# Gated delta-rule block: k turned to token rows by VectorE's 32x32 transposes and eight DMAs in place of TensorE's products with the identity, with a new order on all engines

## The chip, the cores and the metric

The kernel runs on one core of one Trainium2 chip, as one program. The metric is the device time of one execution in microseconds. Everything is float32.

## The reference

The input x is 16 sequences of 256 tokens by 256 channels. It is normalised over its channels and projected to q, k, v and z (32 heads of 64) and to two gates per head. q, k and v pass a causal convolution of four taps over time. q and k are scaled to unit length. Each head then runs a recurrence over the tokens with a 64x64 state, and the result is normalised, gated and projected back:

```python
def step(Sstate, xs):
    q_t, k_t, v_t, g_t, b_t = xs
    Sstate = Sstate * jnp.exp(g_t)[..., None, None]
    kv = jnp.einsum('bhk,bhkv->bhv', k_t, Sstate)
    delta = (v_t - kv) * b_t[..., None]
    Sstate = Sstate + k_t[..., :, None] * delta[..., None, :]
    o_t = jnp.einsum('bhk,bhkv->bhv', q_t, Sstate)
    return (Sstate, o_t)
...
o = o * lax.rsqrt(var + EPS) * norm_weight * jax.nn.sigmoid(z)
return o.reshape(Bsz, Sl, VDIM) @ w_out.T
```

Both the attention part and a gated feed-forward part (256 to 1024 to 256) are normalised and added to their input: `x = x + _layernorm(attn(_layernorm(x)))`, then the same with the feed-forward part.

## The kernel before

Stage 1 normalises x, transposes it and computes the gates. Stage 3 is the feed-forward part. Stage 2, the attention, takes most of the time and is all that the change touches. It has 64 steps: 8 groups of four heads by 8 spans of 512 tokens (two sequences). A step holds 16 tiles of 64 tokens by two head halves (G = 16), on 128 partitions.

In a step TensorE makes eight projections of 128x512 (`project`, L1313; outputs 0 and 1 are k, 2 and 3 are q, 4 and 5 are v, 6 and 7 are z). ScalarE does the first tap from PSUM and VectorE adds three more (`conv`, L1077) for k and v; for q, ScalarE makes the products and GpSimd adds them. k and q then lie with channels on partitions. `scores` (L1335) multiplies k with k and q per tile. The recurrence is done in chunks of 64 tokens, so a 64x64 triangular matrix has to be inverted per tile: VectorE solves its 16x16 diagonal blocks column by column (`substitute`, L1091, after two transfers through DRAM, a_d), and four rounds of small products join them (`join16_inner` to `join_outer`, L1348 to L1382), fed by two more transfers (z_d and x_d).

The chunks follow each other in a chain over c = 0 to 3: `key_state` (TensorE, L1384), `residual` (VectorE, L1145), `solve` (TensorE, L1393), `delta_out` (ScalarE, L933), `advance` (TensorE, L1403), `new_state` (VectorE, L1153), with `output` (L1413) beside them. After the last chunk come `square_o`, `add_squares`, `sum_squares`, `log_var`, `combine`, `gates`, `gated`, `project_out` and `accumulate`. The state starts anew in each step, so no step needs the state of another.

Token rows of k, that is tokens on partitions, are needed for the length of k (`squares`, `sum_k`, `norms`, `columns`) and for `kt`, the left operand of `advance`. In the kernel before they come from `k_tokens` (L1330): 32 products of a 64x64 block with the identity per half of a step, into a PSUM bank of which ScalarE takes squares and VectorE takes `kt`. Token rows of v are made without TensorE: VectorE transposes 32x32 blocks (`turn_v`, L1107, into v_x) and eight DMAs put the blocks in their places (`v_turned`, L712).

The order of the work is written out by hand for each engine in a function `turn(s)`, where s[k] is the step that is k turns old. All engines run their turns in this fixed order, and every dependency is a semaphore wait (`wait_for(eng, sem, step, count, back)`). SyncE issues every DMA, also in a written order (L720), with the waits in between on the same engine. Projections, scores, k_tokens, sum_squares and project_out share four PSUM banks (`ring`, L550); the others have banks of their own. `ap_mat`, `kt`, `z_t`, `v_r` and `q_g` are double, `gcrow`, `xT`, `k_tok` and `v_x` are single.

## Time and profile before

| | |
|---|---|
| time, median of 3 runs | 3149.84 us (3148.64 to 3151.75) |
| the profiled execution: its own time | 3143.98 us |
| its span, first to last instruction | 3142.2 us |
| VectorE busy | 2390.4 us (76%) |
| ScalarE busy | 1765.5 us (56%) |
| GpSimd busy | 1117.6 us (36%) |
| SyncE's DMA queue, share of 16 engines | 34.9% |
| mean granted TensorE clock | 0.988 |

The engine rows are sums of busy time over the whole span, so they mix the three stages. Granted clock 1.0 is 2.4 GHz and 0.5 is 1.2 GHz. TensorE's own row stands further down with the rows that the prediction uses.

### The profile page before, as it was taken

What the parts mean: (1) busy time and instruction counts of PE and PEld (TensorE: products, weight loads), DVE (VectorE), ACT (ScalarE), POOL (GpSimd) and SP (SyncE); (2) the same over time, 40 slices, a digit from 0 to 9 for tenths busy, and PEclk for the clock granted to TensorE, in tenths of its full rate; (3) what the DMA queues carried; (4) which work ended last, traced back from release to release, by engine and by line L of the source; (5) the groups of instructions that cost most, each with busy time, mean ns of one, the idle gap of its engine ahead of it and who ended that gap; (6) DMA issues with size and microseconds to landing.
All of it is one profiled execution on the core that took longest, in us unless ns stands there. A gap on an engine that the chain in (4) does not pass through costs nothing. (4 is left out here: it accounts for less than half of the span.)

```text
span 3142.2 us, 109422 instructions
## 1 busy us (share of the span) xinstructions
PE 3023.2 (96%) x46912; PEld 2040.8 (65%) x46912; DVE 2390.4 (76%) x5674; ACT 1765.5 (56%) x3306; POOL 1117.6 (36%) x904
## 2 busy tenths in 40 slices
PE   6799999999999999999999999999999999789998
PEld 3466666666666666666666666666766666655455
DVE  7578888888788878888878888887888888545644
ACT  5456666665666655666656566665566666333432
POOL 1444444444444444444444444444444444100000
PEclk9899999999999999999999999999999999899999
DMA  5333434344344433433344444333333334300000
GB/s 152 69 62 68 79 65 68 68 86 70 70 70 83 68 68 64 82 63 66 69 85 69 70 70 86 67 67 67 73 69 64 67 69 69 75 14 27 27 21 14
DMA packets 1027793, 208.77 MB, mean 66 GB/s; under 512 B 977904, under 2 KB 998768, under 8 KB 1026160
## 3 DMA queue, kind: packets, MB, share of 16 engines
q1 hardware_dynamic: 1027312, 201.78, 34.9%
q8 instruction: 373, 6.11, 0.8%
q14 instruction: 108, 0.88, 0.1%
HBM read 120.13 MB, written 39.58 MB: 51 GB/s over the span
## 5 line engine op out<-in xcount | busy, mean ns | idle before, releaser
L1317 PE MATMUL bank<-xT,w_sb 128*128 128x512 f32 x2048 | 996.9, 615 | 15.7 <-DVE kq L1082 9.2
L1317 PEld LDWEIGHTS bank<-xT,w_sb 128*128 128x128 f32 x2048 | 359.7, 190 | 355.9 <-issue 311.9
L773 POOL TENSOR_TENSOR kq<-kq,product 128x510 f32<-128x510 f32 (+2 forms) x384 | 437.3, 1146 | 108.9 <-ACT kq L869 94.3
L1082 DVE SCALAR_TENSOR_TENSOR v_c<-bank,cw,v_c 128x510 f32<-128x510 f32 (+2 forms) x384 | 286.3, 746 | 23.0 <-ACT v_c L869 13.1
L1082 DVE SCALAR_TENSOR_TENSOR kq<-bank,cw,kq 128x510 f32<-128x510 f32 (+2 forms) x384 | 283.7, 739 | 23.7 <-ACT kq L869 14.6
L761 POOL TENSOR_TENSOR dec_ap<-gcrow,gcb 128x1024 f32<-128x1024 f32 x64 | 121.8, 1903 | 502.4 <-DMA gcb<-gcb_d 502.4
L1342 PE MATMUL bank<-kq 64*64 64x128 f32 x4096 | 277.9, 270 | 3.4 <-DVE ap_mat L1135 1.9
L1446 PE MATMUL bank<-wo,u_sq 128*128 128x256 f32 x1024 | 261.4, 399 | 11.4 <-DVE u_sq L1168 11.4
L1097 DVE TENSOR_TENSOR prod_un<-a_un,x_un 128x15 f32<-128x15 f32 (+7 forms) x960 | 216.1, 225 | 60.3 <-DMA a_un<-a_d 42.2
L873 ACT ACTIVATE product<-bank,cw 128x512 f32<-128x512 f32 x384 | 257.1, 688 | 2.1 <-PE bank L1317 2.1
L1424 PEld LDWEIGHTS bank<-ap_mat,delta 64*64 64x64 f32 x4096 | 218.3, 135 | 47.0 <-issue 47.0
L777 POOL TENSOR_SCALAR z_tmp<-z_tmp 128x512 f32<-128x512 f32 x128 | 79.2, 619 | 469.4 <-ACT z_tmp L863 464.0
L1424 PE MATMUL bank<-ap_mat,delta 64*64 64x64 f32 x4096 | 243.2, 220 | 0.0
L934 ACT COPY delta<-bank 128x256 f32<-128x256 f32 x256 | 95.4, 373 | 260.4 <-PE bank L1399 260.4
L1342 PEld LDWEIGHTS bank<-kq 64*64 64x64 f32 x4096 | 228.2, 133 | 5.6 <-issue 5.6
L1101 DVE TENSOR_TENSOR x_un<-x_un,prod_un 128x15 f32<-128x15 f32 (+7 forms) x960 | 201.0, 209 | 32.9
L869 ACT ACTIVATE kq<-bank,cw 128x512 f32<-128x512 f32 x256 | 176.9, 691 | 79.5 <-PE bank L1317 77.9
L1446 PEld LDWEIGHTS bank<-wo,u_sq 128*128 128x128 f32 x1024 | 188.3, 194 | 39.2 <-DVE u_sq L1168 12.5
L1422 PE MATMUL bank<-q_g,state 64*64 64x64 f32 x3072 | 199.5, 221 | 1.1 <-ACT delta L934 1.1
L786 POOL TENSOR_TENSOR q_g<-kq,gcrow 128x512 f32<-128x512 f32 x128 | 188.5, 1494 | 0.8 <-PE bank L1424 0.6
L1422 PEld LDWEIGHTS bank<-q_g,state 64*64 64x64 f32 x3072 | 186.4, 134 | 1.5 <-issue 1.3
L1389 PEld LDWEIGHTS bank<-state,kq 64*64 64x64 f32 x3072 | 112.0, 135 | 98.6 <-issue 98.6
(169 smaller groups left out, 5767.3 us busy)
## 6 DMA issues: line engine op xcount, KB each, us to landing
xT<-xT_d SPq DMA_DIRECT2D x64, 512.0 KB, 3.9
gcrow<-gcrow_d SPq DMA_DIRECT2D x128, 256.0 KB, 4.4
v_r<-v_x SPq DMA_DIRECT2D x512, 64.0 KB
a_d<-ap_mat SPq DMA_DIRECT2D x256, 64.0 KB, 3.6
z_t<-z_d SPq DMA_DIRECT2D x256, 64.0 KB, 2.5
w_sb<-in_w_qkvz SPq DMA_DIRECT2D x8, 1024.0 KB, 6.6
x_un<-eye_un SPq DMA_DIRECT2D x64, 128.0 KB, 2.2
a_un<-a_d SPq DMA_DIRECT2D x64, 128.0 KB, 3.5
```

Of the source, the lines that this page charges most:

```text
L773: nc.gpsimd.tensor_tensor(t[:, :, d:SEQ], t[:, :, d:SEQ], prod[:, :, 0:SEQ - d], ALU.add).then_inc(tap_added[i], 1)
L786: ins = nc.gpsimd.tensor_tensor(q_g[m.par][:, a * GP:(a + 1) * GP, :], half_of(m, 1)[:, a, :].rearrange("p (g c) -> p g c", c=C), gcrow[:, ...
L869: nc.scalar.activation(dst, bank[:, :], ACT.Identity, scale=cw_two[m.grp % 2][:, s * TAPS + TAPS - 1:s * TAPS + TAPS]).then_inc(tap_done[s ...
L873: ins = nc.scalar.activation(products[i % 4], bank[:, :], ACT.Identity, scale=cw_two[m.grp % 2][:, w:w + 1])
L1082: ins = nc.vector.scalar_tensor_tensor(t[:, :, d:SEQ], src[:, :, 0:SEQ - d], cw_two[m.grp % 2][:, w:w + 1], t[:, :, d:SEQ], ALU.mult, ALU.add)
L1097: own.need(own.mark(nc.vector.tensor_tensor(prod, a_un[:, j + 1:B, j:j + 1].broadcast_to([P, rows, wid]), x_un[:, j:j + 1, 0:wid].broadcas ...
L1101: ins = nc.vector.tensor_tensor(rest, rest, prod, ALU.subtract)
L1317: ins = nc.tensor.matmul(bank[:, :], w_two[m.grp % 2][:, h, s * P:(s + 1) * P], xT[:, h, :], start=(h == 0), stop=(h == HT - 1))
L1342: ins = nc.tensor.matmul(bank[half, i * P:(i + 1) * P], kq[half, k, s // 2, t0:t0 + C], kq[half, k:q + 1:q - k, s // 2, t0:t0 + C], start= ...
L1422: nc.tensor.matmul(o, state[c % 2][half, i, :], q_g[m.par][half, g, :], start=True, stop=False)
L1424: ins = nc.tensor.matmul(o, delta[half, i, :], p_t[m.par][half, g, :], start=(c == 0), stop=True)
L1446: ins = nc.tensor.matmul(bank[:, t * HID:(t + 1) * HID], u_sq[:, a, (2 * k + t) * P:(2 * k + t + 1) * P], wo[m.grp % 2][:, a, :], start=(a ...
```

## The change

k's token rows are made as v's are. `turn_k` transposes 32x32 blocks of k on VectorE into `k_tok`, and `k_turned` moves the blocks with eight DMAs into a new tile `k_r`. `squares` and `scale_k` read `k_r` in SBUF, and `squares`, `sum_k`, `scale_k` and `scale_v` each take a whole step in one instruction in place of two halves. `tokens` and `k_tokens` are gone from TensorE. `v_x` is gone too: v's blocks also pass through `k_tok`, so `turn_k` waits until v's DMAs of the step before have landed. `substitute` is split into its product and its subtraction. The order of every engine is new: the pipeline spans six turns (DEPTH) in place of four, and load_gates, x_out and identity_in stand elsewhere in SyncE's order. In the diff below, indentation is cut by 16 and lines left out are marked.

```diff
         prod_un = sb("prod_un", [P, 4 * B])
         x_row = sb("x_row", [P, G, C])
-        v_x = sb("v_x", [P, G, C])
+        k_r = sb("k_r", [P, G, C])
         p16 = sb("p16", [P, G, W2])
         x_top = sb("x_top", [P, G, W2])
         p1 = sb("p1", [P, G, W2])
...
-        DEPTH = 4
+        DEPTH = 6
...
-            return banks[(18 * m.off + place) % 4]
+            return banks[(2 * m.off + place) % 4]
...
+    def turned(dst, landed):
+
         for h in range(2):
             for f in range(2):
                 for t in range(2):
                     r, q = D * h + W2 * t, D * h + W2 * f
+                    sp.dma_start(dst[r:r + W2, :, W2 * f:W2 * f + W2], k_tok[q:q + W2, :, W2 * t:W2 * t + W2]) \
+                        .then_inc(landed, 16)
+
+    def v_turned(m):
+        turned(v_r[m.par], v_f_in)
+
+    def k_turned(m):
+        turned(k_r, k_f_in)
 
     def turn(s):
+        if s[5]:
+            wait_for(sp, mats_done[0], s[5], 1)
+            units_out(s[5])
+        if s[4]:
+            wait_for(sp, qg_done[0], s[4], 1, back=1)
+            load_gates(s[4])
+        if s[5]:
+            wait_for(sp, a_d_out, s[5], 64)
+            units_in(s[5])
+            wait_for(sp, vx_done[0], s[5], 1)
+            v_turned(s[5])
+        if s[4]:
+            wait_for(sp, kx_done[1], s[4], 1)
+            k_turned(s[4])
+        if s[5]:
+            wait_for(sp, zt_done, s[5], 1)
+            z_out(s[5])
+            x_out(s[5])
+            wait_for(sp, z_d_out, s[5], 16)
+            z_back(s[5])
+            wait_for(sp, x_d_out, s[5], 16)
+            x_back(s[5])
+        if s[3]:
+            wait_for(sp, proj_full[4], s[3], 1, back=1)
+            load_x(s[3])
+        if s[4]:
+            identity_in(s[4])
...
-    def squares(m, a, bank):
-        nc.scalar.activation(k_tok[:, a * GP:(a + 1) * GP, :], bank[:, :].rearrange("p (g c) -> p g c", c=C), ACT.Square).then_inc(ksq_done[a], 1)
+    def squares(m):
+        nc.scalar.activation(k_tok[:, :, :], k_r[:, :, :], ACT.Square).then_inc(ksq_done, 1)
...
-        ins = nc.vector.transpose(v_x[:, a * GP:(a + 1) * GP, :].rearrange("p g c -> p (g c)"), v_c[:, a, :])
+        ins = nc.vector.transpose(k_tok[:, a * GP:(a + 1) * GP, :].rearrange("p g c -> p (g c)"), v_c[:, a, :])
...
+    def turn_k(m, a):
+        ins = nc.vector.transpose(k_tok[:, a * GP:(a + 1) * GP, :].rearrange("p g c -> p (g c)"), half_of(m, 0)[:, a, :])
+        if a in kx_done:
+            ins.then_inc(kx_done[a], 1)
+
+    def sum_k(m):
+        nc.vector.tensor_reduce(sumk, k_tok[:, :, :], AX.X, ALU.add).then_inc(sumk_done, 1)
+
+    def scale_k(m):
+        nc.vector.tensor_tensor(kt[m.par][:, :, :], k_r[:, :, :], col(e_tail).broadcast_to([P, G, C]), ALU.mult).then_inc(kt_done, 1)
+
+    def scale_v(m):
+        nc.vector.tensor_tensor(v_r[m.par][:, :, :], v_r[m.par][:, :, :], col(br).broadcast_to([P, G, C]), ALU.mult).then_inc(vr_done, 1)
...
+        if s[4]:
+            wait_for(dve, ks_full[1], s[4], 1)
+            residual(s[4], 1)
+        if s[3]:
...
+        if s[4]:
...
+        if s[3]:
...
+        if s[5]:
+            wait_for(dve, op_full[0], s[5], 1)
+            accumulate(s[5], 0, ring(s[5], 2))
+        if s[3]:
...
+            sub_rest(s[3], 14)
+            wait_for(dve, v_f_in, s[3], 128)
+            scale_v(s[3])
+        if s[4]:
+            wait_for(dve, st_full[1], s[4], 1)
...
+            new_state(s[4], 1)
+            wait_for(dve, state_done[1], s[4], 1)
...
+            wait_for(dve, ks_full[2], s[4], 1)
+            residual(s[4], 2)
+        if s[2]:
...
+            conv(s[2], 4, ring(s[2], 0))
+        if s[5]:
+            wait_for(dve, op_full[1], s[5], 1)
+            accumulate(s[5], 1, ring(s[5], 3))
+        if s[4]:
+            wait_for(dve, st_full[2], s[4], 1)
+            new_state(s[4], 2)
+        if s[2]:
+            wait_for(dve, ksq_done, s[2], 1)
+            sum_k(s[2])
+        if s[4]:
+            wait_for(dve, ks_full[3], s[4], 1)
+            residual(s[4], 3)
+        if s[2]:
+            wait_for(dve, rk_done, s[2], 1)
+            wait_for(dve, rhs_done[3], s[2], 1, back=2)
+            columns(s[2])
+            conv(s[2], 5, ring(s[2], 2))
+            wait_for(dve, score_full[1], s[2], 1)
+            wait_for(dve, deca_done, s[2], 1)
+            wait_for(dve, o_full[3], s[2], 1, back=2)
+            matrices(s[2], 1, ring(s[2], 3))
+            wait_for(dve, score_full[2], s[2], 1)
+            matrices(s[2], 2, ring(s[2], 0))
+            wait_for(dve, score_full[3], s[2], 1)
+            matrices(s[2], 3, ring(s[2], 2))
+            matrices(s[2], 0, ring(s[2], 1))
+        if s[4]:
...
+            add_squares(s[4], 1)
...
+            add_squares(s[4], 0)
+        if s[2]:
+            scale_k(s[2])
+            turn_v(s[2], 1)
+            turn_v(s[2], 0)
+        if s[3]:
+            wait_for(dve, z16_done, s[3], 1)
+            turn_back(s[3])
+        if s[4]:
...
+            combine(s[4], 1, ring(s[4], 1))
+        if s[1]:
...
+            conv(s[1], 0, ring(s[1], 0))
+        if s[4]:
...
+            combine(s[4], 0, ring(s[4], 0))
         if s[1]:
...
             conv(s[1], 1, ring(s[1], 1))
+        if s[4]:
...
+            gated(s[4], 1)
...
+            gated(s[4], 0)
+        if s[2]:
+            wait_for(dve, x_un_in, s[2], 16)
+            wait_for(dve, a_un_in, s[2], 16)
+            sub_product(s[2], 0)
...
+            sub_rest(s[2], 6)
         if s[1]:
+            wait_for(dve, conv_done[0], s[1], 1)
+            wait_for(dve, v_f_in, s[1], 128, back=1)
+            turn_k(s[1], 0)
+            wait_for(dve, conv_done[1], s[1], 1)
+            turn_k(s[1], 1)
+        if s[2]:
+            sub_product(s[2], 7)
+        if s[3]:
+            wait_for(dve, st_full[0], s[3], 1)
+            new_state(s[3], 0)
+        if s[2]:
...
         if s[1]:
+            wait_for(dve, gc_in, s[1], 48)
+            tail(s[1])
+        if s[2]:
+            sub_product(s[2], 10)
...
-    def tokens(src, a, bank):
...
-    def k_tokens(m, a, bank):
...
+        if s[2]:
+            wait_for(pe, conv_done[1], s[2], 1)
+            project(s[2], 3, ring(s[2], 1))
+        if s[4]:
...
+            advance(s[4], 0)
+            wait_for(pe, qg_done[0], s[4], 1)
+            wait_for(pe, og_done[0], s[4], 1, back=1)
+            output(s[4], 0)
+            wait_for(pe, state_done[0], s[4], 1)
+            key_state(s[4], 1)
+        if s[5]:
+            wait_for(pe, z_exp[1], s[5], 1, back=-3)
+            wait_for(pe, og_done[0], s[5], 1)
+            project_out(s[5], 0, ring(s[5], 2))
+        if s[2]:
...
+            project(s[2], 6, ring(s[2], 3))
+        if s[4]:
+            wait_for(pe, rhs_done[1], s[4], 1)
+            solve(s[4], 1)
+        if s[2]:
+            wait_for(pe, z_exp[1], s[2], 1)
+            wait_for(pe, acc_done[0], s[2], 1, back=3)
+            project(s[2], 4, ring(s[2], 0))
+        if s[4]:
...
+            advance(s[4], 1)
+            output(s[4], 1)
+            wait_for(pe, state_done[1], s[4], 1)
+            key_state(s[4], 2)
+        if s[5]:
...
+            project_out(s[5], 1, ring(s[5], 3))
+        if s[4]:
+            wait_for(pe, rhs_done[2], s[4], 1)
+            solve(s[4], 2)
+        if s[2]:
...
+            wait_for(pe, z_exp[0], s[2], 1)
+            scores(s[2], 1, ring(s[2], 3))
+        if s[4]:
...
+            advance(s[4], 2)
+        if s[2]:
...
+            wait_for(pe, conv_done[4], s[2], 1)
+            scores(s[2], 2, ring(s[2], 0))
+        if s[4]:
+            wait_for(pe, state_done[2], s[4], 1)
+            key_state(s[4], 3)
+        if s[2]:
+            scores(s[2], 0, ring(s[2], 1))
+        if s[4]:
+            output(s[4], 2)
+            wait_for(pe, rhs_done[3], s[4], 1)
+            solve(s[4], 3)
+        if s[3]:
+            wait_for(pe, z_in, s[3], 64)
+            join16_inner(s[3])
+        if s[4]:
...
+            output(s[4], 3)
+        if s[2]:
+            wait_for(pe, conv_done[5], s[2], 1)
+            scores(s[2], 3, ring(s[2], 2))
+        if s[3]:
...
+            wait_for(pe, x_row_in, s[3], 64)
+            join16_outer(s[3])
         if s[1]:
...
+            wait_for(pe, mats_done[3], s[1], 1, back=1)
+            project(s[1], 0, ring(s[1], 0))
+        if s[4]:
...
+            sum_squares(s[4], 1, ring(s[4], 1))
+        if s[3]:
...
+            join_inner(s[3])
+        if s[4]:
...
+            sum_squares(s[4], 0, ring(s[4], 0))
         if s[1]:
+            project(s[1], 1, ring(s[1], 1))
+        if s[3]:
...
+            join_outer(s[3])
         if s[1]:
+            wait_for(pe, mats_done[0], s[1], 1, back=1)
+            wait_for(pe, comb_done[1], s[1], 1, back=3)
+            project(s[1], 2, ring(s[1], 3))
+            wait_for(pe, conv_done[0], s[1], 1)
+            project(s[1], 7, ring(s[1], 0))
+            wait_for(pe, comb_done[0], s[1], 1, back=3)
+            project(s[1], 5, ring(s[1], 2))
+        if s[3]:
...
+            solve(s[3], 0)
```

## Rows read from the trace of the kernel before

**Rows 1.** The page's busy times: us, share of the span, instructions.

```profile
PE 3023.2 (96%) x46912; PEld 2040.8 (65%) x46912; DVE 2390.4 (76%) x5674; ACT 1765.5 (56%) x3306; POOL 1117.6 (36%) x904
```

**Rows 2.** Windows: stretch, its length, busy us per engine, clock, DMA share, GB/s.

```profile
1200.00:1500.00 300.00, 298.79 (x5303) 208.36 (x5299) 244.63 (x570) 180.39 (x337) 131.05 (x105) 1.00 0.41 73
```

**Rows 3.** TensorE's timeline: start, duration, instruction; projections 0 and 2 of two steps.

```profile
196.15 3.60 PE L1317 MATMUL bank<-xT,w_sb 128*128 128x512 f32 x8
...
2646.23 3.60 PE L1317 MATMUL bank<-xT,w_sb 128*128 128x512 f32 x8
```

**Rows 4.** TensorE's timeline, parts of one turn in the middle.

```profile
1402.38 1.10 PE L1326 MATMUL bank<-masks,kq 64*64 64x64 f32 x32
1403.31 0.33 PE L1422 MATMUL bank<-q_g,state 64*64 64x64 f32 x4
...
1404.71 1.15 PE L1326 MATMUL bank<-masks,kq 64*64 64x64 f32 x32
1405.65 0.68 PE L1409 MATMUL bank<-delta,kt 64*64 64x64 f32 x16
1406.11 0.33 PE L1422 MATMUL bank<-q_g,state 64*64 64x64 f32 x4
...
1417.00 1.13 PE L1439 MATMUL bank<-u_sq,ones 128*128 128x512 f32 x2
1418.05 1.63 PE L1362 MATMUL bank<-p,x_row 64*48 64x32 f32 x64
1419.61 1.12 PE L1439 MATMUL bank<-u_sq,ones 128*128 128x512 f32 x2
1420.57 3.60 PE L1317 MATMUL bank<-xT,w_sb 128*128 128x512 f32 x8
1424.10 1.20 PE L1371 MATMUL bank<-z_t,ap_mat 32*32 32x32 f32 x64
...
1430.82 1.98 PE L1317 MATMUL bank<-xT,w_sb 128*128 128x512 f32 x4
1432.73 0.68 PE L1409 MATMUL bank<-delta,kt 64*64 64x64 f32 x16
1433.35 1.98 PE L1317 MATMUL bank<-xT,w_sb 128*128 128x512 f32 x4
...
1461.13 3.60 PE L1317 MATMUL bank<-xT,w_sb 128*128 128x512 f32 x8
```

**Rows 5.** TensorE's timeline at the end of stage 2, with idle time and releaser.

```profile
2737.94 0.68 PE L1409 MATMUL bank<-delta,kt 64*64 64x64 f32 x16 [0.56 <-ACT delta L934]
2739.22 0.68 PE L1389 MATMUL bank<-state,kq 64*64 64x64 f32 x16 [0.61 <-DVE state L1158]
```

**Rows 6.** Groups of VectorE: count, busy us, mean ns, idle us before.

```profile
L1124 DVE TENSOR_TENSOR v_r<-v_r,cols 128x512 f32<-128x512 f32 x128 | 106.1, 829 | 0.0
L1108 DVE STREAM_TRANSPOSE v_x<-v_c 128x512 f32<-128x512 f32 x128 | 89.6, 701 | 0.0
L1685 DVE TENSOR_TENSOR acc<-gcrow,dec_ap 128x1024 f32<-128x1024 f32 x7 | 8.6, 1225 | 0.7
```

**Rows 7.** Timelines of VectorE and GpSimd: scale_v's two halves, and mask.

```profile
1441.92 0.68 DVE L1124 TENSOR_TENSOR v_r<-v_r,cols 128x512 f32<-128x512 f32 x1
...
1450.88 0.98 DVE L1124 TENSOR_TENSOR v_r<-v_r,cols 128x512 f32<-128x512 f32 x1
...
1448.96 2.35 POOL L765 TENSOR_TENSOR dec_ap<-dec_ap,masks 128x1024 f32<-128x1024 f32 x1 [0.78 <-ACT dec_ap L853]
```

**Rows 8.** SyncE's timeline: DMA issues (start, duration, count).

```profile
1425.13 6.93 SPq L717 DMA_DIRECT2D v_r<-v_x  x8
...
1486.73 0.40 SPq L697 DMA_DIRECT2D z_d<-t_un  x1
1489.89 2.87 SPq L702 DMA_DIRECT2D z_t<-z_d  x4
1492.88 0.54 SPq L684 DMA_DIRECT2D x_un<-eye_un  x1
```

**Rows 9.** A window in which v's transfers end, columns as in rows 2.

```profile
1433.00:1433.50 0.50, 0.50 (x17) 0.43 (x12) 0.04 (x1) 0.50 (x2) 0.00 (x0) 1.00 0.23 34
```

578 lines of the change are left out of this document (188 added, 390 removed).

## The prediction, made before the changed kernel ran

> **What bounds the kernel now.** I read the page's busy times first: TensorE is busy for 96% of the span, VectorE for 76% [rows 1]. An average over three stages proves little, so next the windows: in a stretch in the middle of stage 2 TensorE is busy 298.79 of 300 us at granted clock 1.00 (2.4 GHz), VectorE 244.63, ScalarE 180.39, GpSimd 131.05, the DMA engines 41% [rows 2]. Then TensorE's timeline. Projections 0 and 2 stand side by side once per turn, so their start marks the turn: from 196.15 to 2646.23 lie 60 turns [rows 3], 2450.08 / 60 = 40.83 us each. An undisturbed one takes 1461.13 - 1420.57 = 40.56 [rows 4]; 0.27 a turn is lost to late arrivals. Nothing but TensorE's own work fills a turn, so what shortens TensorE's turn shortens the kernel, until another engine or a transfer is late.
>
> **What goes from TensorE.** Ends of products are modelled and overlap the next start, so I count from start to start. One k_tokens call: 1403.31 - 1402.38 = 0.93; the other 1405.65 - 1404.71 = 0.94 [rows 4]. Together 1.87 us a turn, and VectorE, ScalarE or a DMA must carry them.
>
> **What the new order saves on TensorE.** Wide products (128 rows by 256 or 512 columns) and small ones cost extra where they alternate. A lone projection takes 1432.73 - 1430.82 = 1.91. sum_squares alone takes 1418.05 - 1417.00 = 1.05, and sum_squares followed by two projections 1424.10 - 1419.61 = 4.49, against 1.05 + 2 x 1.91 = 4.87 apart: each join of two wide calls saves 0.19. On the other side of the border, advance takes 1433.35 - 1432.73 = 0.62 ahead of a wide call and 1406.11 - 1405.65 = 0.46 ahead of a small one: 0.16 more. So a wide run fewer is worth 0.35 us [rows 4]. The order before has ten wide runs a turn: projections 7, 3, 5, 6, 4 alone, projection 1, two project_out, sum_squares(1), and sum_squares(0) with projections 0 and 2. The new one has seven: projection 3; project_out(0) with 6; 4; project_out(1); 0 with sum_squares(1); sum_squares(0) with 1; 2 with 7 and 5. Three fewer, 1.05 us. Bounds: nothing, if project_out ahead of a projection doesn't pipeline as the row shows, and 1.35, if a pair saves 2 x 1.91 - 3.53 = 0.29 by itself.
>
> **What the new order adds on TensorE.** The chunk chain has two places where little stands between. With nothing between but output(0), key_state(1) must follow advance(0) by 2739.22 - 2737.94 = 1.28 us, since new_state(0) lies between [rows 5]. The old order had projection 7 there. The new one has only output(0), so advance 0.46 and output about as much, 0.92: a stall of 0.36, at most 0.5. For the other chunks I find cover: project_out(0) and projection 6 (3.6 us) over residual(1), projection 4 over delta_out(1), output(1) with its double products over new_state(1), project_out(1) over residual(2), scores over delta_out(2) and new_state(2).
> TensorE's turn then is 40.56 - 1.87 - 1.05 + 0.36 = 38.00 us.
>
> **VectorE.** Its busy time is 244.63 / 300 x 40.83 = 33.3 us a turn [rows 2]. Added: two transposes of 0.70, 1.40 [rows 6]. sum_k, scale_k and scale_v each become one instruction of 1024 columns. The nearest row with two SBUF operands of that width is 1.225 us, against two halves of 0.68 (0.83 for scale_v on average) [rows 6, 7]: about -0.13, -0.13 and -0.4. New busy time 34.0, with some 1.2 us between dependent instructions (my estimate) 35.2 of 38.0. That is tight: it leaves 2.8 us, and the order fixes where. VectorE waits for TensorE's chunk products (new_state(1), residual(2), new_state(2)) and, through o_full(3), for output(3) ahead of matrices(1): each holds some 0.3 to 1.1 us of it. From matrices(1) on VectorE runs without a wait through add_squares, scale_k, turn_v, turn_back, two conv, gated, seven columns of substitute and turn_k to new_state(0), on which key_state(1) waits. I put this loop (output(3), that row of VectorE's work, new_state(0), key_state(1) to output(3)) at 37.9 us, from the mean durations, give or take 0.4. So it ties with TensorE's own turn, and a lengthening there counts whole. I take +0.3 for it: 38.3. Bounds: 0, and +1.5 in the second rival.
>
> Here the rows speak of a port. scale_v's second half, started while mask ran on GpSimd (1448.96 for 2.35 us), took 0.98; its first half, with GpSimd idle, 0.68 [rows 7]. The Trainium skill (SBUF — State Buffer, SBUF: two separate sides) says that a VectorE instruction with two SBUF inputs and a GpSimd instruction that reads SBUF exclude each other for a whole instruction. By that rule, the trace agrees: mask ended at 1451.31, and the half ended 0.55 later. The rule speaks against the change, since scale_k read PSUM before and reads k_r in SBUF now; what it would do is the second rival.
>
> **ScalarE and GpSimd** have room: 180.39 / 300 x 40.83 = 24.6 and 17.8 us of 38 [rows 2]. squares becomes one 1024-wide call. It stands behind the wait for k_f_in, with delta_out(2), first_tap(5) and norms queued behind it, so a late k stops the chunk chain within 1 us.
>
> **SyncE and the DMAs.** v's eight take 6.93 us to issue, 1425.13 to 1432.06 [rows 8], and the engines are emptied by about 1433.3, since the share falls to 0.23 in the half microsecond from 1433.0 [rows 9]: 1.3 us after the issue. k's eight are alike: 8.2 us from kx_done to k_f_in. turn_k stands right ahead of new_state(0), and squares some 10.5 us later on ScalarE (behind TensorE's key_state(1), two wide runs of 3.6 and 1.9 and two small calls, and four ScalarE calls): 2 us to spare. turn_k also waits for v's DMAs, which read k_tok; I get them landed about 1 us before it. Behind k's eight on SyncE stand z_out, x_out, z_back, x_back, load_x and identity_in. From turn_k: 6.9 for the issue, 0.4 for z_out, 1489.89 - 1486.73 - 0.40 = 2.8 until it has landed, 2.9 for z_back [rows 8], some 2 to land, together 15.0. TensorE reaches join16_inner about 17 us after turn_k. Slack 2 us, cost 0. load_gates now stands between units_out and units_in: its three issues fall into the 3 us or so in which a_d lands, and a_un has about 1 us to spare before column 0; I cost it at nothing, and if that cover goes, each microsecond is one of VectorE's loop. The split of substitute changes no instruction. SyncE's own issue time grows by 6.9 to some 31 us with its waits, under 38. DMA share rises from 0.41 x 40.83 = 16.7 us of a turn to some 20 of 38.3 (estimate: eight DMAs of v took about 5 us at two thirds share).
>
> **Sum.** Turn 38.3, plus the 0.27 of late arrivals that I keep: 38.6. Gain 40.83 - 38.6 = 2.23, x 60 turns = 134 us. Filling and emptying the pipeline: a step waits on the same chain, k adds some 8 us of DMA beside a path that had room, and the first and last turns lose projections that they hadn't filled; I take +3 (bounds -8 and +20). 3143.98 - 134 + 3 = 3013 for the profiled execution. The median is 5.86 above the profiled one: 3019.
>
> **Rival 1, TensorE's order pays less and VectorE's loop binds.** Nothing from the wide runs (+1.05) gives a turn of 39.05, plus 0.27: 39.3, gain 1.5 x 60 = 92, time 3061. For: VectorE with 35.2 of 38 us leaves no room to reorder. Against: the 0.38 saved by a run of three is on the row.
>
> **Rival 2, the port.** scale_k and scale_v wait behind GpSimd instructions of 1.5 to 2.4 us, and conv and add_squares beside scale_q and differences. If 1.5 us of it falls in VectorE's loop: turn 37.9 + 1.5 = 39.4, plus 0.27, gain 1.16 x 60 = 70, time 3083. Against: scale_v stood in such a place and lost only 0.3 [rows 7].
>
> **Rival 3, slower: SyncE's order.** k's DMAs stand between turn_k and z_out. If the chain from turn_k to join16_inner grows from 15 us by more than its slack of 2, TensorE stands at z_in, join16_outer or ScalarE at k_f_in, each turn. It decides from 2 + (40.83 - 38.6) = 4.2 us more: then the kernel is no faster. With 6 us more (the chain 40% longer, the issue of eight DMAs held up by a ring that now serves 20 us of 38) the turn is 42.6, time 3143.98 + 1.8 x 60 + 6 = 3258. For: v's issues took 6.93 / 8 = 0.87 each and z_back's 2.87 / 4 = 0.72, so issues of the same size do get held up [rows 8]. Against: the DMA engines stay half idle.
>
> **Chances.** The forecast, 2995 to 3050: 0.58. Rivals 1 and 2, 3050 to 3105: 0.27. Below 2995: 0.06. Rival 3: 0.07. No change, when a wait I haven't seen eats the gain: 0.02. A change under 0.2% (6.3 us) can't be told from none. Faster 0.91, same 0.02, slower 0.07. Range 2990 to 3100.
>
> **What would show it.** Projection 0 to projection 0 some 38.6 us apart. Seven wide runs and no identity products. project_out(0) with projection 6 in 3.6 us start to start. An idle of about 0.4 before key_state(1) by new_state(0), and none above 0.3 elsewhere on TensorE. VectorE busy near 0.89 of a turn, transposes x256. scale_k at 1.2 us; 2 or more speaks for the port. squares waiting for k_r's DMA, or join16_inner for z_t's, speaks for rival 3. I am wrong if the turn is above 39 with TensorE waiting at a place not named here.

## The result, and the profile after

| | before | after |
|---|---|---|
| time, median | 3149.78 us (4 runs) | 3102.52 us (4 runs, 3101.71 to 3114.59) |
| ratio | | 0.9858, 95% interval 0.9834 to 0.9883 |
| span of the profiled execution | 3142.2 us | 3100.4 us |
| from join_inner to join_inner on TensorE, mean of 63 turns | 40.68 us | 40.21 us |
| TensorE idle "issue", 200 to 2600 us | 7.7 us | 60.4 us |

The kernel is 47 us faster where I forecast 131. The time lies 2.5 us outside my range.

The page's busy times of the changed kernel, which answer to [rows 1]:

```profile
PE 2889.3 (93%) x42816; PEld 1955.3 (63%) x42816; DVE 2436.7 (79%) x5610; ACT 1753.3 (57%) x3242; POOL 1103.5 (36%) x904
```

The window that answers to [rows 2], columns as there:

```profile
1200.00:1500.00 300.00, 286.84 (x4752) 197.13 (x4751) 254.70 (x588) 186.37 (x338) 123.90 (x101) 1.00 0.52 86
```

TensorE, busy 298.79 of 300 us before, now stands idle for 13 of 300. The turn's mark has to be another one, since projections 0 and 2 no longer stand side by side: join_inner. Its first and its last start in the changed kernel's timeline of TensorE, then those of the kernel before:

```profile
152.70 1.20 PE L1382 MATMUL bank<-z_t,ap_mat 32*32 32x32 f32 x64
2685.98 1.01 PE L1382 MATMUL bank<-z_t,ap_mat 32*32 32x32 f32 x52 [0.60 <-ACT z_t L918]
```

```profile
157.66 1.20 PE L1371 MATMUL bank<-z_t,ap_mat 32*32 32x32 f32 x64
2720.25 1.20 PE L1371 MATMUL bank<-z_t,ap_mat 32*32 32x32 f32 x64 [0.67 <-ACT z_t L912]
```

So 5.0 us are gained ahead of the first, 29.3 in 63 turns (2562.59 against 2533.28 us), and 7.5 of the 41.8 us of span behind the last.

A turn with hardly a stall (38.37 us), TensorE's timeline of the changed kernel, answers to [rows 4]:

```profile
713.95 1.20 PE L1382 MATMUL bank<-z_t,ap_mat 32*32 32x32 f32 x64
715.08 1.12 PE L1450 MATMUL bank<-u_sq,ones 128*128 128x512 f32 x2
716.04 1.88 PE L1342 MATMUL bank<-xT,w_sb 128*128 128x512 f32 x4
...
718.98 5.42 PE L1342 MATMUL bank<-xT,w_sb 128*128 128x512 f32 x12
724.33 0.68 PE L1410 MATMUL bank<-v_r,z_t 64*64 64x64 f32 x16
...
726.86 0.68 PE L1420 MATMUL bank<-delta,kt 64*64 64x64 f32 x16
727.37 0.63 PE L1435 MATMUL bank<-ap_mat,delta 64*64 64x64 f32 x16
728.16 0.68 PE L1400 MATMUL bank<-state,kq 64*64 64x64 f32 x16 [0.15 <-DVE state L1170]
728.77 1.99 PE L1457 MATMUL bank<-wo,u_sq 128*128 128x256 f32 x8
730.60 1.88 PE L1342 MATMUL bank<-xT,w_sb 128*128 128x512 f32 x4
732.41 0.68 PE L1410 MATMUL bank<-rhs,z_t 64*64 64x64 f32 x16
...
738.92 0.68 PE L1410 MATMUL bank<-rhs,z_t 64*64 64x64 f32 x16
...
744.45 1.63 PE L1364 MATMUL bank<-z_t,ap_mat 64*48 64x32 f32 x64
...
747.97 1.65 PE L1373 MATMUL bank<-p,x_row 64*48 64x32 f32 x64
749.55 1.98 PE L1342 MATMUL bank<-xT,w_sb 128*128 128x512 f32 x4
```

The wide runs and the missing identity products are as forecast: three projections side by side take 724.33 - 718.98 = 5.35, project_out(0) with projection 6 takes 732.41 - 728.77 = 3.64. Between filling and draining lie 60 whole turns, from 190.80 to 2612.24 us in the changed kernel and from 199.68 to 2649.76 before. The shortest of them takes 38.04 us after (it starts at 1561.41) and 40.56 before. The mean is 40.36 after, 2.32 above the shortest, and 40.83 before, 0.27 above. So the shortest turn became 2.52 us shorter and the mean turn only 0.47. What is new lies between shortest and mean.

I took each call's mean time from its start to the next start, less the shortest such time. The largest differences are join16_outer 0.60, output(0) up to key_state(1) 0.41, solve(3) up to join16_inner 0.29, join16_inner 0.29, output(3) 0.21 and projection 0 0.18. All but the second belong to the stretch from 738.92 to 749.55 in the rows above, or stand right behind it. It is 10.6 us of small products (12 with the idles of a mean turn) between project_out(1) and projection 0, with no wide product in it. In the order before, the longest such stretch was 6.7 us.

The table of waits of TensorE, 200 to 2600 us (line waiting, what it waits for, us in total, times, longest), of the changed kernel:

```profile
PE bank L1400 <- DVE state L1170: 33.5, 60, 2.4
PE bank L1373 <- issue: 25.6, 25, 1.8
PE bank L1364 <- issue: 11.7, 19, 2.1
PE bank L1364 <- DMA z_t<-z_d: 10.6, 12, 1.4
```

and of the kernel before, its two longest:

```profile
PE bank L1353 <- issue: 5.7, 11, 0.8
PE bank L1389 <- DVE state L1158: 1.3, 1, 1.3
```

"issue" is an idle for which the profile shows no releaser, and here the releaser can be found among the transfers. The chip fetches TensorE's instructions in pieces of 16 KB on a queue of their own, q8. One such idle, in TensorE's timeline of the changed kernel (join16_outer, L1373):

```profile
583.72 0.68 PE L1373 MATMUL bank<-p,x_row 64*48 64x32 f32 x22
585.24 1.17 PE L1373 MATMUL bank<-p,x_row 64*48 64x32 f32 x42 [0.84 <-issue]
```

The windows over it (PE's column is the first with a count; the last three numbers are granted clock, DMA share, GB/s), and the transfers of q8 in the half microsecond from 582.5 (count, MB, share):

```profile
583.50:584.00 0.50, 0.50 (x21) 0.50 (x18) 0.50 (x2) 0.50 (x2) 0.50 (x1) 1.00 0.00 0
584.00:584.50 0.50, 0.41 (x19) 0.29 (x13) 0.50 (x2) 0.18 (x1) 0.50 (x2) 1.00 0.00 0
584.50:585.00 0.50, 0.00 (x0) 0.00 (x0) 0.50 (x1) 0.00 (x0) 0.50 (x1) 1.00 0.00 0
```

```profile
q8 instruction: 1, 0.02, 12.1%
```

That fetch ran from 583.00 to 583.96, by its record in the trace. No operand was missing, no other transfer ran (share 0.00), and TensorE went on 1.28 us after the fetch had ended. It is the same each time. The changed kernel has 63 "issue" idles of 0.25 us or more in that stretch, and they ended 1.15 to 1.62 us after the end of a fetch, while fetches come only about five times a turn (q8: 304 in 2400 us; between the starts of two, the trace has 257 products and weight loads in the median). The kernel before has 15 such idles, at 1.28 to 1.58 us.

So TensorE runs out of instructions. One fetched piece lasts about 3 us among the joins' products (join16_outer's 128 instructions, weight loads included, pass in 1.56 us). The fetches ahead of these idles were no slower than the others: 1.11 us on average, against 1.15 for all. But from the start of such a fetch TensorE went on for only 1.6 us and 92 products and weight loads (medians), and what was fetched came into use about 2.5 us behind that start. Why such a fetch does not start earlier, the trace doesn't show.

### The profile page after: what moved, and what is told of

The parts are those of the page before. It is cut to its first block and busy times, and to the rows that moved or that the text cites. A ratio compares the mean times of both kernels' runs of the same rounds, so it can differ in the third digit from the quotient of the medians.

```text
span 3100.4 us, 101425 instructions
## 1 busy us (share of the span) xinstructions
PE 2889.3 (93%) x42816; PEld 1955.3 (63%) x42816; DVE 2436.7 (79%) x5610; ACT 1753.3 (57%) x3242; POOL 1103.5 (36%) x904
## 5 line engine op out<-in xcount | busy, mean ns | idle before, releaser
L1342 PE MATMUL bank<-xT,w_sb 128*128 128x512 f32 x2048 | 980.5, 612 | 9.7 <-PEq L516 5.2
L784 POOL TENSOR_TENSOR kq<-kq,product 128x510 f32<-128x510 f32 (+2 forms) x384 | 449.2, 1183 | 717.4 <-ACT kq L873 707.4
L1342 PEld LDWEIGHTS bank<-xT,w_sb 128*128 128x128 f32 x2048 | 372.5, 192 | 374.5 <-issue 346.9
L879 ACT ACTIVATE product<-bank,cw 128x512 f32<-128x512 f32 x384 | 249.2, 684 | 6.8 <-PE bank L1342 2.8
L1147 DVE TENSOR_TENSOR ap_mat<-bank,dec_ap 128x512 f32<-128x512 f32 x256 | 160.1, 684 | 115.9 <-PE bank L1435 108.9
L1115 DVE TENSOR_TENSOR x_un<-x_un,prod_un 128x15 f32<-128x15 f32 (+7 forms) x960 | 220.5, 230 | 28.7
L1106 DVE TENSOR_TENSOR prod_un<-a_un,x_un 128x15 f32<-128x15 f32 (+7 forms) x960 | 214.5, 223 | 25.6 <-DMA a_un<-a_d 3.4
L797 POOL TENSOR_TENSOR q_g<-kq,gcrow 128x512 f32<-128x512 f32 x128 | 160.5, 1276 | 30.9 <-PE bank L1435 28.0
L1420 PEld LDWEIGHTS bank<-delta,kt 64*64 64x64 f32 x3072 | 108.9, 135 | 98.3 <-issue 98.2
```

Of the source, the lines that this page charges most:

```text
L784: nc.gpsimd.tensor_tensor(t[:, :, d:SEQ], t[:, :, d:SEQ], prod[:, :, 0:SEQ - d], ALU.add).then_inc(tap_added[i], 1)
L797: ins = nc.gpsimd.tensor_tensor(q_g[m.par][:, a * GP:(a + 1) * GP, :], half_of(m, 1)[:, a, :].rearrange("p (g c) -> p g c", c=C), gcrow[:, ...
L879: ins = nc.scalar.activation(products[i % 4], bank[:, :], ACT.Identity, scale=cw_two[m.grp % 2][:, w:w + 1])
L1106: last_prod[:] = own.mark(nc.vector.tensor_tensor(prod, a_un[:, j + 1:B, j:j + 1].broadcast_to([P, rows, wid]), x_un[:, j:j + 1, 0:wid].br ...
L1115: ins = nc.vector.tensor_tensor(rest, rest, prod, ALU.subtract)
L1342: ins = nc.tensor.matmul(bank[:, :], w_two[m.grp % 2][:, h, s * P:(s + 1) * P], xT[:, h, :], start=(h == 0), stop=(h == HT - 1))
```

## The experiments

The turn is the mean over 63 turns. "key_state(1)" is TensorE's idle before it and "issue" all its idles of that name, both in us from 200 to 2600. Each kernel was timed in three rounds. In the diffs indentation is cut, and `.then_inc` calls, the lines `if s[k]:` and most waits are left out.

| run | median us | ratio to before, 95% | turn | key_state(1) | issue |
|---|---|---|---|---|---|
| the change | 3102.5 | 0.9834 to 0.9883 | 40.21 | 33.5 | 60.4 |
| k_dma_small | 3095.5 | 0.9819 to 0.9866 | 40.05 | 32.3 | 59.0 |
| old_plus_8_dmas | 3146.2 | 0.9987 to 1.0010 | 40.74 | 0.8 | 5.4 |
| join16_half_instr | 3051.8 | 0.9674 to 0.9731 | 39.36 | 22.6 | 29.6 |
| old_without_k_products | 3107.6 | 0.9860 to 0.9896 | 40.20 | 0.5 | 20.9 |
| both_join16_half_instr | 3041.8 | 0.9659 to 0.9688 | 39.29 | 29.5 | 9.0 |
| new_state_before_turn_k | 3143.7 | 0.9976 to 1.0011 | 40.82 | 80.4 | 52.8 |
| joins_spread | 3124.7 | 0.9913 to 0.9952 | 40.39 | 55.8 | 34.5 |
| joins_spread_new_state_first | 3167.7 | 1.0058 to 1.0100 | 40.95 | 67.1 | 48.0 |
| columns_first_no_q_adds | 3073.0 | 0.9742 to 0.9805 | 39.73 | 9.3 | 62.7 |
| new_state_at_once | 3115.2 | 0.9872 to 0.9918 | 40.49 | 9.8 | 70.5 |
| joins_half_new_state_at_once | 3082.3 | 0.9775 to 0.9813 | 39.95 | 9.2 | 23.1 |
| joins_spread_new_state_at_once | 3138.8 | 0.9965 to 0.9989 | 40.68 | 12.4 | 57.2 |
| v_from_k_r | 3070.1 | 0.9739 to 0.9791 | 39.75 | 10.4 | 61.3 |
| v_from_k_r_state_first | 3086.0 | 0.9782 to 0.9854 | 39.95 | 13.4 | 68.8 |
| joins_half_v_from_k_r | 3054.0 | 0.9690 to 0.9729 | 39.47 | 16.1 | 22.2 |
| accumulate_early | 3081.6 | 0.9758 to 0.9814 | 40.07 | 9.2 | 79.9 |
| joins_half_v_from_k_r_alone | 3029.4 | 0.9603 to 0.9648 | 39.07 | 12.9 | 10.5 |
| joins_half_v_from_k_r_no_q_adds | 3026.8 | 0.9603 to 0.9638 | 39.03 | 10.7 | 9.1 |

### Is it the DMA load?

k_dma_small, on the changed kernel:

```diff
-def turned(dst, landed):
+def turned(dst, landed, n=W2):
...
-    sp.dma_start(dst[r:r + W2, :, W2 * f:W2 * f + W2], k_tok[q:q + W2, :, W2 * t:W2 * t + W2]) \
+    sp.dma_start(dst[r:r + n, :, W2 * f:W2 * f + W2], k_tok[q:q + n, :, W2 * t:W2 * t + W2]) \
...
-    turned(k_r, k_f_in)
+    turned(k_r, k_f_in, 1)
```

> The changed kernel, but each of k's eight DMAs moves 1 partition of 32 (k_r is filled with 0.1 once), so issues, waits and order stay and their load on the DMA engines goes. The changed kernel's turn of TensorE is 40.2 us where its own products need 37.9; 1.0 us of the rest is idle put down to no engine, at join16_inner, join16_outer and near them. Theory F (TensorE waits there for its own instructions, since the new order puts 12 us of small products in a row): the idles stay, turn 39.6 to 40.2, time within 30 us of the changed kernel's 3102. Theory D (k's transfers load the DMA engines, so z_t, x_row or the instruction fetches come late): the idles go, turn 38.2 to 38.8, time 3000 to 3030.

old_plus_8_dmas, on the kernel before:

```diff
             v_turned(s[3])
+            v_turned(s[3], k_tok, more_in)
```

> The kernel before, with eight more DMAs like v's (v_x into k_tok, at a time when k_tok is free) behind v's on SyncE; nothing else. Theory F: the old order has wide products between the small ones, so the turn stays within 0.3 us of 40.85 and the time within 20 us of 3150. Theory D: z_t, x_row and fetches come late as in the changed kernel, turn 41.8 or more, time 3200 or more.

Both say no. Without 31 of 32 parts of k's transfers the idles stay (32.3 and 59.0 us), and the kernel before carries eight more transfers a turn at no cost. The 7 us between 3102.5 and 3095.5 lie within what the intervals leave open. If they are real, they may be z_t's: TensorE's waits for its transfer fell from 10.6 to 4.5 us.

### Is it the number of instructions in the stretch?

join16_half_instr, and both_join16_half_instr with the same edit in join16_inner too:

```diff
-    for g in range(G):
+    for g in range(0, G, 2):
         for h in range(2):
             half = slice(D * h, D * h + D)
-            ins = nc.tensor.matmul(banks[5][D * h:D * h + 3 * B, g * W2:(g + 1) * W2], x_row[half, g, 0:3 * B],
-                                   p16[half, g, :], start=True, stop=True)
+            w = g // 4 * 4
+            ins = nc.tensor.matmul(banks[5][D * h:D * h + 3 * B, w * W2:(w + 4) * W2], x_row[half, g, 0:3 * B],
+                                   p16[half, w:w + 4, :], start=True, stop=True)
```

> The changed kernel, but join16_outer makes 16 products of 128 columns in place of 32 of 32 columns (wrong blocks): half the instructions, and by scores' rate (0.87 us for 8 x 2 of 128 columns) 1.7 us of work in place of 1.56. Theory F: fewer instructions in the dense stretch, the idle of 0.75 us at join16_outer goes at least by half, turn 39.5 to 39.9, time 3060 to 3085. Theory D: nothing is gained, the turn grows by 0.2 us, time 3105 to 3120.

> The changed kernel with join16_inner and join16_outer each issued as 16 products of 128 columns in place of 32 of 64 (other blocks are multiplied, so this is only a time): the same columns, 128 instructions fewer a turn in TensorE's unbroken stretch of small products. Fetch theory (TensorE runs out of fetched instructions in that stretch): the idles of TensorE put down to its own issue at both joins, 25.6 + 11.7 + 6.9 us in the window 200 to 2600, nearly go, the granted clock falls less often, a turn takes 39.0 to 39.5 in place of 40.2, the time is 3020 to 3050, below the 3052 with join16_outer alone halved. Rival (the products themselves got cheaper): join16_outer's shortest time from start to start is well below the 32-product one and the idles stay; then join16_inner halved brings another 0.3 us a turn with the idle before it unchanged.

There is a slip in the second of these texts: a call is 32 products of 32 columns (the rows count each as two), not of 64, and becomes 16 of 128. So TensorE has twice the columns to pass. The shortest join16_outer took 1.88 in place of 1.56 us, join16_inner 1.75 in place of 1.42, and the shortest turn 38.65 in place of 38.04. The kernel became 51 us faster with one call halved, more than I had expected, and 61 us with both, as expected. The waits of both_join16_half_instr that answer to the list above:

```profile
PE bank L1402 <- DVE state L1170: 29.5, 61, 1.4
PE bank L1365 <- DMA z_t<-z_d: 5.5, 5, 1.5
...
PE bank L1365 <- issue: 2.1, 4, 0.7
...
PE bank L1375 <- issue: 1.1, 2, 0.7
```

The idles go with the instructions, though the products got dearer. The rival of cheaper products is out. The granted clock, which fell to half nine times between 200 and 2600 us in the changed kernel, stayed at 1.00 here from 200 to 2592 us.

old_without_k_products, on the kernel before, leaves out 14 of the 16 products of each half of k_tokens:

```diff
-    for i in range(GP):
+    for i in range(1):
```

> The kernel before in its own order, with k_tokens cut from 16 products a half to 2 (kt and the squares then read a stale bank), so what the removal alone is worth to TensorE is seen. If TensorE's products bind there as I summed: 1.87 - 0.12 = 1.75 us a turn less, turn 39.1, time about 3040. If a chain over VectorE or ScalarE takes over, or fetches come late because 64 fewer products bring the small ones closer, the gain is under 1.2 us a turn and the time above 3075.

It gives 38 us (3145.6 to 3107.6 in the same rounds) and not 105. Two waits took the place of most of the products, in its table of waits of TensorE:

```profile
PE bank L1409 <- ACT delta L934: 26.1, 59, 0.8
PE bank L1353 <- issue: 15.8, 23, 1.5
```

The identity products had covered ScalarE's delta_out ahead of advance. From start to start this costs 0.63 us of every turn, more than the 0.44 a turn that the table shows as idle, since the ends of products are modelled, and the starving ahead of join16_inner grew too. Removed alone, the products would have brought nearly what the whole change did (the two intervals overlap). The new order's covers for the chunk chain work: this wait doesn't stand in the changed kernel's table.

joins_spread splits the stretch, on the changed kernel (join16_outer with 0 and 1 does 8 of the 16 tiles each):

```diff
-    join16_outer(s[3])
+    join16_outer(s[3], 0)
     project(s[1], 0, ring(s[1], 0))
-    sum_squares(s[4], 1, ring(s[4], 1))
-    join_inner(s[3])
-    sum_squares(s[4], 0, ring(s[4], 0))
+    join16_outer(s[3], 1)
+    sum_squares(s[4], 1, ring(s[4], 1))
+    sum_squares(s[4], 0, ring(s[4], 0))
+    join_inner(s[3])
     project(s[1], 1, ring(s[1], 1))
```

with ScalarE's and VectorE's calls moved to fit.

> The changed kernel with the unbroken stretch of small products broken up: join16_outer in two halves of 8 tiles on either side of projection 0, sum_squares(1) and (0) side by side ahead of join_inner, projection 1 alone (8 wide runs a turn in place of 7, which costs 0.35 us a turn by the rows). Same instructions on every engine, ScalarE and VectorE reordered to fit. Fetch theory: the idle before join16_outer's parts falls from 25.6 us to under 10, the clock falls less often, turn 39.6 to 39.9, time 3060 to 3085. Rival (the idles have another cause, or the stretch before the split is long enough by itself): the idle stays near 25 us and the added wide run costs 0.35 x 60 = 21 us, time near 3122.

The fetch theory was right on the place and I was wrong on the time: join16_outer's idle fell from 25.6 to 7.4 us, and the kernel became 22 us slower. That the rival's 3122 was met is chance, since the idle didn't stay. The shortest turn is 38.52, 0.48 above, which I put down to the eighth wide run (0.35 in my sum). And VectorE's new order made it late at new_state(0), 55.8 us against 33.5, with turn_k waiting for v's DMAs in 38 turns in place of 22.

### What makes new_state(0) late?

new_state_before_turn_k and, with the spread joins, joins_spread_new_state_first:

```diff
-    turn_k(s[1], 0); turn_k(s[1], 1)
     sub_product(s[2], 7)
-    new_state(s[3], 0)
     sub_rest(s[2], 7)
     sub_product(s[2], 8); sub_rest(s[2], 8)
+    new_state(s[3], 0)
+    turn_k(s[1], 0); turn_k(s[1], 1)
```

> The changed kernel with one move in VectorE's order: substitute's columns 7 and 8 and new_state(0) ahead of turn_k, in place of turn_k ahead of them. No instruction more or less. If VectorE's lateness at new_state(0) costs what TensorE's idle before key_state(1) shows (33.5 us over 60 turns, bimodal 0.15 and 1.1 us), that idle falls to about 10 us, a turn is 0.3 to 0.4 us shorter and the time 3075 to 3082. Rival (the idle there only gives the instruction fetch time to run ahead, so what is saved there is lost again at join16_outer): the idle before key_state(1) falls, those at join16_inner and join16_outer grow, and the time stays within 8 us of 3100. Second rival: turn_k is later by some 1 us, k's DMAs and z_back with it, and TensorE waits for z_t before join16_inner in more than 12 turns.

> Both edits together: join16_outer split around projection 0, and new_state(0) ahead of turn_k. If the two causes add, the turn is shorter than in either alone, 39.2 to 39.5, time 3040 to 3060. If the fetch absorbs what new_state(0) gives, the time is that of the spread joins alone, within 5 us.

Neither text had this: 41 us slower than the changed kernel, with the idle before key_state(1) grown from 33.5 to 80.4, and with the spread joins 43 us slower than those alone. By the rows it should have been half a microsecond earlier a turn. VectorE's timeline of that kernel shows why, and below it GpSimd's:

```profile
736.36 0.22 DVE L1106 TENSOR_TENSOR prod_un<-a_un,x_un 128x64 f32<-128x64 f32 x1
736.62 1.27 DVE L1115 TENSOR_TENSOR x_un<-x_un,prod_un 128x64 f32<-128x64 f32 x1
737.92 1.13 DVE L1106 TENSOR_TENSOR prod_un<-a_un,x_un 128x63 f32<-128x63 f32 x1
739.08 0.23 DVE L1115 TENSOR_TENSOR x_un<-x_un,prod_un 128x63 f32<-128x63 f32 x1
739.23 0.42 DVE L1170 COPY state<-bank 128x256 f32<-128x256 f32 x1
```

```profile
736.54 2.43 POOL L784 TENSOR_TENSOR kq<-kq,product 128x510 f32<-128x510 f32 x2 [4.33 <-ACT kq L873]
```

Two instructions of 64 and 63 columns, 0.22 us elsewhere, take 1.27 and 1.13, each up to about the end of one of GpSimd's two additions of 1.2 us. In the changed kernel turn_k's transposes, which read one tile, stand at that place and lose nothing (0.66 to 0.71 us each, as elsewhere). This is the rule of the port that the prediction cites from the Trainium skill (SBUF — State Buffer, SBUF: two separate sides): a VectorE instruction with two SBUF inputs is locked out until the end of a GpSimd instruction that reads SBUF and had started first. These rows agree, with 1.05 and 0.9 us on 0.22.

columns_first_no_q_adds tests it, on new_state_before_turn_k:

```diff
-    nc.gpsimd.tensor_tensor(t[:, :, d:SEQ], t[:, :, d:SEQ], prod[:, :, 0:SEQ - d], ALU.add)
+    nc.gpsimd.tensor_tensor(t[:, :, d:d + 1], t[:, :, d:d + 1], prod[:, :, 0:1], ALU.add)
```

> The kernel of new_state_before_turn_k (3143.7 us) with GpSimd's additions of q's taps cut to one column each (that part of q is left out); VectorE's order and instructions are untouched. There, two of substitute's instructions of 64 columns took 1.1 to 1.3 us in place of 0.22, each ending with one of GpSimd's 1.2 us additions. Port theory (a VectorE instruction with two SBUF inputs stands while GpSimd's runs, and VectorE's row to new_state(0) is late by it): the two take 0.22 again, TensorE's idle before key_state(1) falls from 80 us to under 20, time 3075 to 3090. Rival (it is the order of the row, GpSimd only happens to run there): the idle and the time stay within 10 us of 3144.

It went as the port theory had it: the products ahead of new_state(0) take at most 0.23 us, the idle is 9.3 us and the time 3073.0, 71 us less than with the additions, in an otherwise unchanged order.

new_state_at_once moves new_state(0) ahead of both turn_k and column 7; joins_half_new_state_at_once and joins_spread_new_state_at_once add it to the halved and to the spread joins:

```diff
+    new_state(s[3], 0)
     turn_k(s[1], 0); turn_k(s[1], 1)
     sub_product(s[2], 7)
-    new_state(s[3], 0)
```

> The changed kernel with new_state(0) right behind substitute's column 6, ahead of both turn_k and column 7, so that turn_k's two transposes (one SBUF input) stand where GpSimd adds q's taps and no product of substitute lies ahead of new_state(0). Theory (VectorE's row from matrices(1) to new_state(0), 18.5 us, with TensorE's 19.0 us from key_state(1) to output(3) closes one loop of 38.0 us in which every wait counts): the row is 1.7 us shorter, TensorE's idle before key_state(1) falls from 33.5 us to about 10, turn 39.8 to 39.9, time 3075 to 3085; the rest of the loss, TensorE's own idles at the joins, stays. Rival: turn_k 1 to 2 us later moves k's eight DMAs and z_back, join16_inner waits for z_t in most turns, and the time stays near 3100.

> new_state(0) right behind column 6, and both join16 calls as 16 products of 128 columns (other blocks are multiplied): both causes taken away at once. If these two are all that stands between the measured turn and my forecast, the turn is 38.49 (sum of the shortest) + 0.4 = 38.9 and the time 3042 - 0.37 x 63 = about 3019, 3012 to 3028. If a third cause of a size that counts is left, the time stays above 3035.

> join16_outer split around projection 0 (the spread joins, 3124.7 us), with new_state(0) right behind column 6. There the idle before key_state(1) had grown to 55.8 us and ate what the spread gave. With VectorE early the turn is 40.88 - 0.85 = 40.0, time 3075 to 3090, about that of new_state_at_once: the spread gives 0.5 of starvation and pays 0.5 in an eighth wide run. If it is under 3070 the spread is worth having; if above 3100, what it does elsewhere costs too.

All three missed. The idle fell to 9 to 12 us as said, and another stood in its place, the third cause that two of the texts had left open. In new_state_at_once:

```profile
PE bank L1341 <- DVE acc L1187: 43.3, 52, 0.9
...
PE bank L1399 <- DVE state L1170: 9.8, 58, 1.1
```

Projection 4 (L1341) waited for the PSUM bank that accumulate(0) frees, since turn_k now stood ahead of it. In the other two this wait is about as long. accumulate_early puts accumulate(0) right behind residual(1):

```diff
     residual(s[4], 1)
+    accumulate(s[5], 0, ring(s[5], 2))
     sub_rest(s[3], 10)
     decay_state(s[4], 1)
...
-    accumulate(s[5], 0, ring(s[5], 2))
```

> new_state_at_once (3115.2 us) with accumulate(0) right behind residual(1), ahead of decay_state(1) and of substitute's columns 11 and 12. There, projection 4 waited for accumulate(0) in 52 of 60 turns, 43.3 us. Theory (a lengthening of 1.3 us between new_state(0) and accumulate(0), and nothing else, ate the gain): that wait falls under 10 us and the time to 3072 to 3085. Rival (turn_k 1.8 us later costs by SyncE's queue): the wait falls, another on z_t or t_un grows, time 3100 or more.

It went as the theory said (3081.6, no wait for accumulate left among TensorE's), 34 us less.

### What holds turn_k?

In the changed kernel 23 of 60 turns have more than 0.3 us of idle before key_state(1), 27.9 of the 33.5 us. In 18 of these 23 turn_k had waited for v's DMAs, and in 4 of the other 37. One of them, VectorE's timeline, then GpSimd's and TensorE's:

```profile
560.82 1.30 DVE L1127 STREAM_TRANSPOSE k_tok<-kq 128x512 f32<-128x512 f32 x2 [1.23 <-DMA v_r<-k_tok]
562.04 0.26 DVE L1106 TENSOR_TENSOR prod_un<-a_un,x_un 128x64 f32<-128x64 f32 x1
562.23 0.41 DVE L1170 COPY state<-bank 128x256 f32<-128x256 f32 x1
```

```profile
559.79 2.43 POOL L784 TENSOR_TENSOR kq<-kq,product 128x510 f32<-128x510 f32 x2 [3.77 <-ACT kq L873]
```

```profile
562.78 0.68 PE L1400 MATMUL bank<-state,kq 64*64 64x64 f32 x16 [1.08 <-DVE state L1170]
```

The port has a part in it. The waits for v's DMAs in these 18 turns were 0.24 to 1.34 us long, but the idle that followed was 1.08 to 1.18 us in 16 of them. And in 18 of the 23 late turns new_state(0) started within 0.03 us of the end of one of GpSimd's additions (562.22 here), in none of the other 37. In 8 of the 60 turns column 7's product, right ahead of new_state(0), took 0.6 to 1.1 us. So it looks as if a short wait sufficed to push column 7's product behind an addition, which then set the length of the idle. No run leaves out the additions in the changed kernel, so this share of the port's is read from rows and not tested.

v_from_k_r has v's blocks pass through k_r (turn_v writes it in place of k_tok), which is free between scale_k and k's DMAs:

```diff
-def turned(dst, landed):
+def turned(src, dst, landed):
...
-    turned(v_r[m.par], v_f_in)
+    turned(k_r, v_r[m.par], v_f_in)
...
-    turned(k_r, k_f_in)
+    turned(k_tok, k_r, k_f_in)
...
+    wait_for(sp, v_f_in, s[4], 128, back=1)
     wait_for(sp, kx_done[1], s[4], 1)
     k_turned(s[4])
...
     add_squares(s[4], 1)
+    scale_k(s[2])
     wait_for(dve, usq_done[0], s[4], 1)
     add_squares(s[4], 0)
-    scale_k(s[2])
+    wait_for(dve, kt_done, s[2], 1)
     turn_v(s[2], 1)
     turn_v(s[2], 0)
...
-    wait_for(dve, v_f_in, s[1], 128, back=1)
     turn_k(s[1], 0)
```

> The changed kernel with v's blocks turned into k_r, which is free between scale_k and k's DMAs, in place of k_tok; SyncE waits for v's DMAs ahead of k's, and turn_k no longer waits. Same instructions and transfers; scale_k stands ahead of add_squares(0). Theory (turn_k's wait for v's DMAs, in 22 of 60 turns, 16.6 us, makes new_state(0) late and the loop through VectorE passes it on): the idle before key_state(1) falls from 33.5 to 12 to 20 us, time 3082 to 3092. Rival (TensorE's other idles take it back, or the wait moved to SyncE delays z_back): 3098 to 3106.

> v_from_k_r with new_state(0) one instruction earlier, ahead of column 7's product, which stands behind GpSimd's addition for up to 1.1 us in 8 of 60 turns; turn_k stays ahead of both. Theory: another 5 us to v_from_k_r, idle before key_state(1) near its floor of 9 us, time 3075 to 3087. Rival (the row was not late there once v is out of it): equal to v_from_k_r.

v_from_k_r takes 3070.1 us. That is 32 less than the change, a larger gain than I expected, by the expected cause: the idle before key_state(1) is 10.4 us. It is faster than both kernels, and the version to keep. Its waits of TensorE:

```profile
PE bank L1376 <- issue: 23.6, 24, 3.1
PE bank L1367 <- issue: 12.8, 24, 1.2
PE bank L1356 <- issue: 10.7, 6, 2.9
PE bank L1403 <- DVE state L1171: 10.4, 61, 1.2
```

The starving for instructions is all there still. new_state(0) ahead of column 7's product on top of it did not help (3086.0, and the two intervals overlap). Solve(1) comes no later than before, but projection 4 behind it, which waits for accumulate(0), comes 0.20 us later a turn, mostly in idles too short for the table of waits. That column 7's product, now behind new_state(0) and beside GpSimd's addition, makes accumulate(0) late is my reading. That the edit harms is likely, not shown.

joins_half_v_from_k_r puts that kernel together with the halved joins, joins_half_v_from_k_r_alone leaves the move of new_state(0) out, and joins_half_v_from_k_r_no_q_adds cuts GpSimd's additions too:

> v_from_k_r_state_first with both join16 calls as 16 products of 128 columns (other blocks are multiplied): starvation, v's wait and the port taken away together, and nothing moved that accumulate(0) needs. If these are all, the turn is 38.9 to 39.1 and the time 3042 less 15 to 22, 3020 to 3027, the forecast of 3019 within its own slack. If a wait that I haven't named takes their place, the time stays above 3035.

> v_from_k_r (3070.1 us) with both join16 calls as 16 products of 128 columns (other blocks are multiplied), VectorE's order otherwise that of v_from_k_r. Theory (two causes that add): the halved joins took 61 us from the changed kernel, v_from_k_r 32; of the 61 some stood in the same turns, so 3042 less 15 to 25 = 3017 to 3027, turn 39.0 to 39.2, no idle of TensorE above 15 us in the window. Rival (a third cause of VectorE's takes the place): time above 3035 with TensorE's idle before key_state(1) above 20 us.

> The same with GpSimd's additions of q's taps cut to one column each (that part of q is left out). Port theory: what of VectorE's row is still stretched goes too, another 5 to 12 us, 3008 to 3020. Rival: VectorE has slack by now and it is equal to the run without this edit, within 4 us.

The first missed, with the move of new_state(0) in it. Without the move the time is 3029.4 (3024.7 to 3034.5), 2.4 above what I expected, with a mean of 39.11 over the 60 turns where the shortest takes 38.65. So with starving and v's wait taken away a turn loses 0.5 us in place of 2.3, and nothing else of size is left. GpSimd's additions are worth nothing there (3026.8, the intervals overlap), as the rival said: VectorE has slack by then.

## Why the prediction was wrong, point by point

**What was right.** The price of TensorE's own turn was right. k_tokens gone, three wide runs fewer and a short stall at key_state(1) made 38.00 in my sum, against 38.04 for the shortest turn. From advance(0) to key_state(1) it took 728.16 - 726.86 = 1.30 us, where I had 1.28 from [rows 5]; the profile shows only 0.15 of it as idle, not my 0.4, since the ends of products are modelled. scale_k took 1.22 and sum_k 1.21 us as said. k's eight DMAs took 5.3 us to issue, less than the 6.93 that I had taken from v's, and 2.3 us each to land, and squares never waited for them. Rival 3, SyncE's order, did show, but small: join16_inner waited for z_t in 12 of 60 turns, 10.6 us.

**The step that failed** is in the sum: "Turn 38.3, plus the 0.27 of late arrivals that I keep: 38.6". I kept the lateness of the order before, with 0.3 for VectorE. Against a turn of 38.0 that is 0.57 of lateness, and it was 2.32. It splits so, in us a turn over 60 turns:

- 1.0 (60.4 us, the rows of the waits named "issue") is TensorE waiting for its own instructions. I counted the wide runs that merge as pure gain. What they left behind is one stretch of 10.6 us of small products, where instructions are used faster than they come. That is the "waiting at a place not named here" of the last part of the prediction.
- 0.33 is the clock. Granted clock was 1.00 throughout this stretch before. After, it fell to half nine times, 41 us in all. Calls that ran in such a spell took 19.6 us longer in total than the shortest of their kind, waits left out. All nine falls came in or within 2 us behind an idle of TensorE's of 1.15 to 2.93 us, seven of them "issue"; there were idles as long without a fall. Here TensorE stood idle for 1.87 us at its own issue, then the clock fell:

```profile
985.00:990.00 5.00, 3.13 (x121) 3.03 (x119) 1.30 (x2) 0.96 (x2) 2.53 (x4) 1.00 0.40 123
990.00:995.00 5.00, 5.00 (x88) 4.27 (x86) 4.60 (x7) 2.45 (x6) 2.51 (x2) 0.62 0.21 32
995.00:1000.00 5.00, 5.00 (x70) 2.40 (x69) 2.72 (x5) 1.53 (x3) 0.00 (x0) 0.70 0.69 139
```

- 0.41 is VectorE late at new_state(0) (33.5 us, less the 0.15 that stands in the shortest turn too), mostly by the wait of turn_k and what GpSimd's addition made of it. "I get them landed about 1 us before it" was wrong in 22 of 60 turns. v's eight took 8.17 us to issue in the median (6.29 to 10.11), where I had 6.93 from [rows 8]; the median before was 6.43. Why they are issued more slowly in the new place I did not test.
- 0.18 is z_t late, as in rival 3.
- The rest, 0.4, is in gaps too small for the list of waits, a good part of them inside the joins. With the halved joins about 0.2 is left of it.

**VectorE's loop.** I put it at 37.9 us. Its shortest was 18.50 from matrices(1) to new_state(0), 0.57 to key_state(1), 18.97 from there to matrices(1): 38.04. The size was right and "runs without a wait" was not: the row held 1.24 us of waits a turn on average (ScalarE's tap 0.5, its gates 0.3, v's DMAs 0.3), and TensorE's half 0.9 us of idles. Both halves are in series, so the loop's mean is 40.37, the turn. A tie between two chains is not worth 0.3 here: each passed the other's lateness on.

**The rivals.** Rivals 1 (3061) and 2 (3083) came nearer than my forecast, but by luck, for they had other reasons. The wide runs paid in full, against rival 1. The port of rival 2 is real but stood elsewhere: scale_k and scale_v took 1.24 and 1.22 us on average and so lost next to nothing, and substitute's short products lost up to 1 us each, next to new_state(0) in 8 of 60 turns. No rival had the instructions.

**Filling and draining.** I took +3 us; it was 12 us less (5.0 and 7.5). That this came out shorter was luck for the forecast. Without it the miss would be larger: 3143.98 - 63 x 0.47 = 3114 for the profiled execution.

**What the forecast was worth.** With most of the starving and v's wait taken away the kernel takes 3029 us, although its joins pass more columns than the changed kernel's (38.65 - 38.04 = 0.61 us a turn, 38 us in all). Without these the time would be about 2991, below the forecast of 3019. This is an estimate from the two shortest turns; no run shows it.

**What stays open.** Spreading the joins cost more, in a wide run and in VectorE's order, than it gave. Why the fetches start so late, and how much of the idle before key_state(1) the port makes in the changed kernel, no run shows. I have not tried an order that breaks up the stretch without an eighth wide run.

## What to carry to other kernels

Price an order not only by the operations that pipeline better side by side, but by what the merging leaves side by side elsewhere: a long stretch of small products can use its instructions faster than they are fetched, and "issue" idles that end a fixed time after a transfer of the instruction queue are the sign. When two chains tie, add up the waits of both, since they come in series. And when an instruction is moved on VectorE, look at what GpSimd does at the new place: here a transpose, with one input, lost nothing there, and a product of two tiles lost about 1 us.

## What the runs showed of the hardware

- TensorE can starve for instructions. In the changed kernel 63 idles of 0.25 us or more ended 1.15 to 1.62 us after a 16 KB fetch. 128 instructions fewer a turn took 51 us of such idles away and 61 us off the time. The Trainium skill (Runtime: NRT & Kernel Launch, Instruction fetch mechanics) says that the sequencer fetches the next 16 KB while it works on the present one and that this is mostly hidden. In the kernel before it is, with 7.7 us of such idles in 2400. In the changed one they are 60.4 us, more than the whole gain of the change, and there the measurement decides.
- The fetches don't suffer from other transfers to an extent that shows: the kernel with k's transfers cut to one partition of 32 kept 59.0 us of such idles, and a fetch took 1.12 us there and 1.15 us in the changed kernel on average.
- A VectorE instruction of 64 columns and two SBUF inputs took 1.27 us in place of 0.22 while GpSimd added two tiles. With the additions cut, new_state_before_turn_k was 71 us faster. A transpose with one SBUF input took its usual 0.66 to 0.71 us beside the same additions.
- The granted clock of TensorE fell to half nine times in the changed kernel, in or within 2 us behind idles of 1.15 to 2.93 us, and this cost about 20 us.
- Eight more SBUF to SBUF transfers of 64 KB a turn cost the kernel before nothing (ratio 0.9987 to 1.0010).
